# Products with values in rounds of eight chunks, for the narrow heads of a fused two-layer transformer kernel

## The chip, the cores and the metric

The kernel runs on one core of a Trainium2 chip. The metric is device time in microseconds (us), the median of several executions. The engines are PE (TensorE: matrix products), DVE (VectorE), ACT (ScalarE), POOL (GpSimd) and SP (SyncE, which issues the DMAs). Results of PE land in eight PSUM banks of 128 partitions by 512 float32; the other engines work mostly in SBUF.

## The reference

Two layers on x of shape (2, 1024, 128), each an attention with 16 heads, a layer norm, and a second block; the last block holds another attention, with heads of width 4:

```
x = layernorm(x + attention0(x))            # causal, heads of width 8
x = layernorm(x + moe0(x))                  # 8 experts, top 2, relu
x = layernorm(x + attention1(x))            # causal, heads of width 8, low rank q and k
# last block: attention2 (not causal), then 8 experts, top 2, gelu
scores = einsum('bhsk,bhtk->bhst', Q[..., :4], K) / sqrt(4)
attn   = softmax(scores); ao = einsum('bhst,bhtv->bhsv', attn, V)    # V of width 4
x = layernorm(x + block(x))
```

## The kernel before

There are 96 heads in order: 0 to 31 are attention 0, 32 to 63 attention 1 (both causal) and 64 to 95 attention 2, the narrow ones (two sequences of 16 heads). Run 0 is heads 0 to 31, followed by the experts of the first layer; run 1 is heads 32 to 95, followed by the experts of the second.

The score matrix of a head (1024 by 1024) is made twice, in chunks of one PSUM bank (128 x 512). `scores_by_query` (L1243, product at L1258) puts queries on the partitions; DVE takes the row maxima from it (`find_max`, L974, reduction at L989). The maxima are negated, split into three bf16 parts on POOL, turned to rows on PE (`max_rows`, L1278) and loaded into the operand of the keys. `scores_by_key` (L1264, product at L1273) makes the scores again with keys on the partitions and the maximum already taken off; ACT writes the exponential to SBUF (L873, into `probs`); `probs_by_v` (L1284, product at L1302) multiplies it by the values of the head, in float32, into one accumulating bank `SUM`. A value operand has 32 columns, so each product fills one of four column quarters of the array, and the quarter is chosen by the chunk's number modulo four; four successive chunks of a narrow head lie side by side in the array. When a group of heads is done (four narrow heads, two or three causal ones), ACT copies `SUM` (`take_sums`), PE turns it (`turn_sums`, L1308, L1312), ACT and POOL gather it and DVE divides it (`normalise`, L999).

A narrow head has 16 chunks, a causal one 9. The query side runs two heads ahead of the key side (`AHEAD`), so head g's loop on PE issues one query product of head g+2 and one key product of head g for each chunk; the pair occupies different rows of the array. Query products go through three banks (`S1`), and a product waits until DVE has reduced the one three before it. Key products go through another three (`S2`) and wait for ACT in the same way. The queues of all engines are written out by hand, in program order; `head` (L1387) is the PE queue of one head. Its 16 chunks stand in four batches of four. After each batch comes a round of products with values, for the four chunks of the batch before: after batch 0 the last round of the head before, after batches 1, 2 and 3 the rounds 0, 1 and 2 of this head. `turn_sums` comes after batch 1 of a head that follows a group's end, ahead of its round; `max_rows` after batch 0, ahead of its round; and other steps of the layers (projections, transposes, routing; the lists `BETWEEN`, L184 to L306) in the middle of a batch, at its second chunk on PE, its third on ACT and DVE.

`probs` has nine places of 512 columns. A narrow head uses eight (`probs_place`, L129); ACT waits before an exponential for the round that read its place last (`pv_before`, L144). The semaphore `pv` counts rounds. The causal heads have two rounds of nine products, over five and four chunks.

Of the kernel before, what the change touches and what calls it, by code (L numbers as in the profile page):

```python
# [14 lines left out]
P = 128  # L15
# [5 lines left out]
NH = B * H  # L21
# [3 lines left out]
CH = 512  # L25
# [17 lines left out]
class Attention:  # L43


    def __init__(self, layer, head_dim, scale_dim, causal):
        self.layer = layer
        self.hd = head_dim
        self.width = H * head_dim
        self.rows = PARTS * PARTS * head_dim  # L50
        self.dv = head_dim + 1

        self.groups = (3, 3, 3, 3, 2, 2) if causal else (4, 4, 4, 4)
        self.scale = float(scale_dim) ** -0.5
        self.causal = causal
        if causal:

            diagonal = [[(i, i, 1) for i in range(4 * c, 4 * c + 4)] for c in range(2)]
            self.by_query = diagonal + [
                [(7, 0, 4)], [(7, 4, 3), (1, 0, 1)], [(6, 0, 4)], [(6, 4, 2), (2, 0, 2)],  # L60
                [(5, 0, 4)], [(5, 4, 1), (3, 0, 3)], [(4, 0, 4)]]
            self.maxima = 3

            self.by_key = [
                [(i, i, 1, 3) for i in range(4)], [(0, 4, 4, 0)], [(1, 4, 4, 1)], [(2, 4, 4, 2)],
# [3 lines left out]
            self.masked = (0, 5)  # L69
            self.batches = [range(0, 5), range(5, 9)]  # L70

            self.pv_order = [
                [(1, 0), (2, 0), (3, 0), (4, 0), (0, 0), (4, 1), (0, 1), (0, 2), (0, 3)],
                [(6, 0), (8, 0), (7, 0), (8, 1), (5, 1), (5, 0), (7, 1), (5, 2), (5, 3)]]
            self.adds = 3
        else:
            self.by_query = [[(i, 4 * c, 4)] for i in range(TB) for c in range(2)]
            self.maxima = 2
            self.by_key = [[(j, 4 * half, 4, 2 * half + j % 2)] for two in range(0, TB, 2) for half in range(2)
                           for j in range(two, two + 2)]  # L80
            self.masked = ()
            self.batches = [range(c, c + 4) for c in range(0, 16, 4)]
            self.pv_order = [[(c, 0) for c in batch] for batch in self.batches]
            self.adds = 1
        self.chunks = len(self.by_key)

# [7 lines left out]
class Head:  # L94
# [32 lines left out]
        return next(k for k, batch in enumerate(self.a.batches) if c in batch)  # L127

    def probs_place(self, c):  # L129
        return c if self.a.causal else c % 8  # L130


HEADS = [Head(g) for g in range(3 * NH)]
RUNS = (range(0, NH), range(NH, 3 * NH))
CHUNKS = [sum(hd.a.chunks for hd in HEADS[:g]) for g in range(3 * NH + 1)]
BATCHES = [sum(len(hd.a.batches) for hd in HEADS[:g]) for g in range(3 * NH + 1)]
GROUP = [sum(hd.ends_group for hd in HEADS[:g]) for g in range(3 * NH + 1)]
GROUPS = [[hd for hd in HEADS if GROUP[hd.g] == i] for i in range(GROUP[-1])]
V_BEFORE = {hd.g: max((o.g for o in HEADS[:hd.g] if o.a.causal == hd.a.causal and o.v_slot == hd.v_slot), default=None)
# [3 lines left out]

def pv_before(g, c):  # L144

    if not HEADS[g].a.causal and c >= 8:
        return BATCHES[g] + (c - 8) // 4 + 1
    if g == 0:
        return 0
    if HEADS[g - 1].a.causal:  # L150
        return BATCHES[g - 1] + HEADS[g - 1].batch_of(c) + 1
    return BATCHES[g - 1] + (c + 8) // 4 + 1


def queries_upto(run, g, c):
# [169 lines left out]
def build(nc, inp, out):  # L325
    ctx = ExitStack()
    with ctx:
        def sb(name, shape, dt=F32):
            return ctx.enter_context(nc.sbuf_tensor(name, shape, dt))
# [18 lines left out]
        qk = sb("qk", [P, RING, 2, S], BF16)  # L348
        v_all = [sb("v8", [P, NH, TB, 9]), sb("v4", [P, NH, TB, 5])]
        v_heads = [sb("v_head8", [P, 6, TB, Q]), sb("v_head4", [P, RING, TB, Q])]  # L350
        probs = sb("probs", [P, 9, CH])
        sums = sb("sums", [P, 2, CH])
        by_quarter = sb("by_quarter", [P, 2, 4, 4, 27])
        pairs = sb("pairs", [P, 4, 27])
# [228 lines left out]
        def _(pool):  # L583
# [79 lines left out]
            def take_v(g):  # L663
                hd = HEADS[g]
                a = hd.a
                if V_BEFORE[g] is not None:
                    pool.wait_ge(sem("pv"), BATCHES[V_BEFORE[g] + 1])
                if a.layer == 0 and hd.n == 0:
                    pool.wait_ge(sem("v_first"), NCH)
                if a.layer > 0 and hd.h == 0:  # L670
                    taken(pool, "v", a.layer, BY_SEQUENCE[hd.b][-1])
                at = a.dv * hd.at_in_group
                nc.gpsimd.tensor_copy(v_head_of(a)[:, hd.v_slot, :, at:at + a.dv], v_of(a)[:, hd.n, :, :]
                                      ).then_inc(sem("v_head"), 1)
# [76 lines left out]
        def _(act):  # L751
# [98 lines left out]
                nc.scalar.activation(neg_rows[:, g % RING, :], neg_ps, ACT.Copy).then_inc(sem("neg_rows"), 1)  # L850

            def take_sums(i):
                act.wait_ge(sem("pv"), BATCHES[GROUPS[i][-1].g + 1])
                ge(act, "out", i - 1)
                nc.scalar.activation(sums[:, i % 2, :], SUM[:], ACT.Copy).then_inc(sem("sums"), 1)

# [323 lines left out]
        def _(pe):  # L1180
# [103 lines left out]
            def probs_by_v(g, k):  # L1284
                hd = HEADS[g]
                a = hd.a
                order = [(c, b, a.by_key[c][b][1] // 4, a.by_key[c][b][3]) for batch in a.pv_order for c, b in batch]
                opens = {next(m for m in order if m[2:] == hq) for hq in {m[2:] for m in order}}
                closes = {next(m for m in reversed(order) if m[2:] == hq) for hq in {m[2:] for m in order}}
                if k == 0:  # L1290
                    pe.wait_ge(sem("v_head"), g + 1)
                    if hd.first_of_group:
                        ge(pe, "sums", GROUP[g])
                pe.wait_ge(sem("probs"), CHUNKS[g] + a.batches[k][-1] + 1)
                for c, b in a.pv_order[k]:
                    if c in a.masked and (c, b) == next(y for y in a.pv_order[k] if y[0] == c):
                        pe.wait_ge(sem("masked"), 2 * g + a.masked.index(c) + 1)
                    j, q0, count, quarter = a.by_key[c][b]
                    at = P * sum(blk[2] for blk in a.by_key[c][:b])
                    half, q = q0 // 4, P * (q0 % 4)  # L1300
                    this = (c, b, half, quarter)
                    ins = mm(SUM[Q * quarter:Q * (quarter + 1), q:q + P * count], v_head_of(a)[:, hd.v_slot, j, :],  # L1302
                             probs[:, hd.probs_place(c), at:at + P * count],
                             start=this in opens and hd.first_of_group, stop=this in closes and hd.ends_group,
                             skip_group_check=True)
                ins.then_inc(sem("pv"), 1)
# [80 lines left out]
            def head(run, g, asked):  # L1387
                hd = HEADS[g]
                for k, batch in enumerate(hd.a.batches):
                    for c in batch:  # L1390

                        upto = min(queries_upto(run, g, c) + 1, CHUNKS[run.stop])
                        for i in range(asked, upto):
                            scores_by_query(i)
                        asked = upto
                        scores_by_key(g, c)
                        before = at_place_before(run, g, k)
                        if c == batch[1] and before is not None:
                            between(before)
                    if k == 0 and g + 1 < run.stop:  # L1400
                        max_rows(g + 1)
                    if k == 1 and g > run.start and HEADS[g - 1].ends_group:
                        turn_sums(GROUP[g - 1])
                    if k > 0:
                        probs_by_v(g, k - 1)
                    elif g > run.start:
                        probs_by_v(g - 1, len(HEADS[g - 1].a.batches) - 1)
                return asked

            def experts(f, last):  # L1410
# [37 lines left out]
            for f, run in enumerate(RUNS):  # L1448
                ge(pe, "y_taken", UNITS * f)
                half_way = CHUNKS[run.start + 1] + HEADS[run.start].a.chunks // 2  # L1450
                asked = CHUNKS[run.start]
                for i in range(asked, half_way):
                    scores_by_query(i)
                max_rows(run.start)
                for i in range(half_way, CHUNKS[run.start + AHEAD] + 1):
                    scores_by_query(i)
                asked = CHUNKS[run.start + AHEAD] + 1
                for g in run:
                    asked = head(run, g, asked)
                last = run.stop - 1  # L1460
                probs_by_v(last, len(HEADS[last].a.batches) - 1)
                experts(f, GROUP[last])


# [68 lines left out]
```

## Time and profile before

| | |
|---|---|
| median of 3 runs | 1196.16 us (1196.11 to 1196.60) |
| the profiled execution: its time, its span | 1196.12 us, 1194.4 us |
| PE, DVE, ACT, POOL busy over the span | 92%, 73%, 65%, 22% |
| mean granted TensorE clock | 0.987 of full |
| narrow heads: from after batch 0 of head 64 to the end of head 93 | 706 to 1042 us |
| heads 94 and 95, without query products beside them | 1042 to 1063 us |
| experts of the second layer | 1063 us to the end |

Times in the rows are us from the start of the span, and durations in us unless marked ns. An instruction's row on PE gives a modelled end and overlaps the next one; the distance from one start to the next is what an instruction takes of the engine. Of a row of the timeline, the first number is its start, the second its duration, "x8" the number of instructions merged into it (a float32 product is recorded as two), and the bracket at its end the idle time before it with what ended it. Some records of products are missing.

### The profile page before, as it was taken

Reading aid. Unit: us, or ns where it says so; the run is one execution under the profiler, and the core shown is the slowest. Engines: PE = TensorE matmul, PEld = TensorE weight load, DVE = VectorE, ACT = ScalarE, POOL = GpSimd, SP = SyncE. Lnnn points to the kernel's source line nnn. Section 1 sums busy time; section 2 is a strip of 40 time slices with the busy share of each in tenths; the row PEclk is TensorE's granted clock in tenths of the full one; section 3 lists DMA queues with packets and bytes.
Section 4 is the critical chain, followed back from the end, with each engine's and each line's share of the span. In section 5 each row is a group of like instructions: output and inputs, shape, how many; then the busy total and the mean of one; then the engine's idle time right before and its main releaser. Section 6 shows DMA issues by size and latency. Waiting matters only on the chain. (4 is left out here: it accounts for less than half of the span.)

```text
span 1194.4 us, 24895 instructions
## 1 busy us (share of the span) xinstructions
PE 1103.6 (92%) x8850; PEld 597.5 (50%) x8850; DVE 871.2 (73%) x2061; ACT 775.9 (65%) x1547; POOL 267.1 (22%) x795
## 2 busy tenths in 40 slices
PE   8999999999999989999988998888889898899996
PEld 5566666656666646666655532222112221136774
DVE  6888878771434487888877889899999989804433
ACT  4576766666444437676676667888888788874443
POOL 4344333331112123433334321011010010100001
PEclk9999999999999999999999999999999999999998
DMA  7345331100003501343221311002111000000000
GB/s 195 82 121 142 101 82 32 42 22 1 1 1 70 121 21 33 98 103 97 61 74 37 60 37 36 18 11 37 37 36 37 11 17 11 7 1 1 10 9 18
DMA packets 39546, 57.65 MB, mean 48 GB/s; under 512 B 9392, under 2 KB 14976, under 8 KB 39040
## 3 DMA queue, kind: packets, MB, share of 16 engines
q1 hardware_dynamic: 39424, 56.06, 19.2%
q8 instruction: 71, 1.16, 0.4%
q14 instruction: 51, 0.42, 0.1%
HBM read 30.81 MB, written 24.64 MB: 46 GB/s over the span
## 5 line engine op out<-in xcount | busy, mean ns | idle before, releaser
L873 ACT ACTIVATE probs<-bank 128x512 f32<-128x512 f32 x1088 | 577.6, 600 | 228.3 <-PE bank L1273 227.3
L989 DVE TENSOR_REDUCE tile_max<-bank 128x1 f32<-128x512 f32 (+3 forms) x1152 | 613.9, 594 | 36.5 <-PE bank L1258 31.2
L1258 PE MATMUL bank<-qk 125*128 125x128 bf16 (+2 forms) x1664 | 389.1, 311 | 49.8 <-DVE tile_max L989 43.9
L1273 PE MATMUL bank<-qk 128*128 128x128 bf16 (+1 forms) x1664 | 385.3, 309 | 5.8 <-ACT probs L873 5.3
L1302 PE MATMUL bank<-probs,v_head 128*32 128x512 f32 (+3 forms) x3328 | 304.0, 454 | 0.1
L1258 PEld LDWEIGHTS bank<-qk 125*128 125x128 bf16 (+1 forms) x1664 | 132.6, 97 | 313.1 <-DVE tile_max L989 240.1
L1156 DVE SCALAR_TENSOR_TENSOR acc<-bank,gate,acc 128x128 f32<-128x128 f32 x256 | 72.0, 344 | 156.7 <-PE bank L1426 156.7
L1302 PEld LDWEIGHTS bank<-probs,v_head 128*32 128x32 f32 x3328 | 139.7, 109 | 53.8 <-issue 31.4
L1273 PEld LDWEIGHTS bank<-qk 128*128 128x128 bf16 (+1 forms) x1664 | 133.2, 97 | 57.6 <-ACT probs L873 22.1
L893 ACT ACTIVATE probs<-bank,sb_b 128x512 f32<-128x512 f32 x128 | 81.0, 684 | 117.9 <-PE bank L1415 117.9
L983 DVE TENSOR_REDUCE tile_max<-bank 128x4 f32<-128x512 f32 x128 | 87.3, 687 | 65.9 <-PE bank L1258 65.2
L1426 PEld LDWEIGHTS bank<-sb_w,probs 128*128 128x128 f32 x1024 | 123.1, 192 | 24.5 <-issue 24.0
L1426 PE MATMUL bank<-sb_w,probs 128*128 128x128 f32 x1024 | 124.7, 275 | 0.0
L1415 PE MATMUL bank<-xT,sb_w 128*128 128x512 f32 x256 | 121.0, 595 | 0.0
L714 POOL TENSOR_SCALAR_AFFINE_SELECT probs<-probs 128x512 f32<-128x512 f32 x128 | 81.2, 634 | 153.7 <-ACT probs L873 153.6
L681 POOL CAST neg_parts<-neg_max 128x8 bf16<-128x8 f32 x96 | 18.2, 189 | 325.8 <-DVE neg_max L996 325.8
L1415 PEld LDWEIGHTS bank<-xT,sb_w 128*128 128x128 f32 x256 | 43.9, 191 | 34.1 <-issue 33.8
L1253 PE MATMUL bank<-mask,ident 128*128 128x512 bf16 x128 | 50.0, 391 | 3.5 <-DVE acc L1156 1.2
L850 ACT ACTIVATE neg_rows<-bank 24x128 bf16<-24x128 bf16 x96 | 24.7, 258 | 22.6 <-PE bank L1281 22.6
L704 POOL TENSOR_TENSOR pairs<-by_quarter 128x108 f32<-128x108 f32 (+1 forms) x24 | 9.4, 393 | 124.1 <-ACT by_quarter L861 124.1
L648 POOL TENSOR_SCALAR rstd<-mean_var 128x4 f32<-128x4 f32 (+1 forms) x12 | 2.8, 236 | 146.9 <-DVE mean_var L1047 146.6
L813 ACT ACTIVATE x<-x_plus,shift,rstd 128x128 f32<-128x128 f32 x64 | 26.2, 488 | 8.3 <-POOL shift L651 8.3
(135 smaller groups left out, 635.6 us busy)
## 6 DMA issues: line engine op xcount, KB each, us to landing
qk<-qk_parts SPq DMA_DIRECT2D x160, 144.0 KB
qk_parts<-q_parts SPq DMA_DIRECT2D x48, 192.0 KB, 2.4
qk_parts<-k_parts SPq DMA_DIRECT2D x48, 192.0 KB, 3.2
qk_parts<-q_parts SPq DMA_DIRECT2D x24, 96.0 KB, 2.3
qk_parts<-k_parts SPq DMA_DIRECT2D x24, 96.0 KB, 2.9
sb_w<-in_w SPq DMA_DIRECT2D x8, 256.0 KB, 3.7
sb_w<-in_w SPq DMA_DIRECT2D x2, 1024.0 KB, 5.9
qk<-neg_rows SPq DMA_DIRECT2D x96, 6.0 KB
```

Source lines behind the costliest of these rows:

```text
L714: nc.gpsimd.affine_select(out=p, in_=p, compare_op=ALU.is_ge, fill=0.0, base=0, pattern=[[0, 4], [1, P]], channel_multiplier=-1).then_inc( ...
L873: nc.scalar.activation(probs[:, hd.probs_place(c), :], S2[i % len(S2)][:], ACT.Exp, scale=hd.a.scale).then_inc(sem("probs"), 1)
L893: nc.scalar.activation(hidden[:, m % 2, fb, :], bank[2 * (m % 2) + fb][:], ACT.Relu if f == 0 else ACT.Gelu, bias=w_sb[f"b1_{f}"][:, FB * ...
L983: ins = nc.vector.tensor_reduce(tile_max[:, hd.slot, 4 * c:4 * c + 4, 0], s1[:].rearrange("p (t k) -> p t k", k=P), AX.X, ALU.max)
L989: ins = nc.vector.tensor_reduce(tile_max[:, hd.slot, t, which:which + 1], s1[:, at:at + P * count], AX.X, ALU.max)
L1156: ins = nc.vector.scalar_tensor_tensor(acc[:, tile, :], Y[m % 2][:, P * t:P * (t + 1)], gate[:, tile, e:e + 1], acc[:, tile, :], ALU.mult, ...
L1253: mm(s1[:], ident16[:], mask16[:].rearrange("p t k -> p (t k)"), start=True, stop=False, skip_group_check=True)
L1258: ins = mm(s1[:, at:at + P * count], qk[hd.query_rows, hd.place, 0, P * t:P * (t + 1)], qk[hd.query_rows, hd.place, 1, P * k0:P * (k0 + co ...
L1273: ins = mm(s2[:, at:at + P * count], qk[hd.key_rows, hd.place, 1, P * j:P * (j + 1)], qk[hd.key_rows, hd.place, 0, P * q0:P * (q0 + count) ...
L1302: ins = mm(SUM[Q * quarter:Q * (quarter + 1), q:q + P * count], v_head_of(a)[:, hd.v_slot, j, :], probs[:, hd.probs_place(c), at:at + P * ...
L1415: ins = mm(bank[2 * (m % 2) + fb][:], w_sb[f"w1_{f}"][:, e, P * fb:P * (fb + 1)], xT[:, tokens(c)], start=True, stop=True)
L1426: ins = mm(Y[m % 2][:, P * t:P * (t + 1)], hidden[:, m % 2, fb, P * t:P * (t + 1)], w_sb[f"w2_{f}"][:, e, fb, :], start=fb == 0, stop=fb = ...
```

## The change

For narrow heads alone, `pv_order` holds two rounds of eight chunks in place of four rounds of four, and `pv_behind` sets where round 0 goes: after batch 2. The other, round 1, goes after batch 0 of the next head (as the causal heads' does already). The causal heads keep their two rounds and their places. `probs` grows from nine to twelve places, and a narrow chunk's place is its number over all narrow heads modulo twelve; `pv_before` follows. `BATCHES`, which counted batches for the semaphore `pv`, becomes `ROUNDS`.

```diff
+            self.pv_behind = 1
...
-            self.pv_order = [[(c, 0) for c in batch] for batch in self.batches]
+
+            self.pv_order = [[(c, 0) for c in range(8 * i, 8 * i + 8)] for i in range(2)]
+            self.pv_behind = 2
...
     def probs_place(self, c):
-        return c if self.a.causal else c % 8
+        return c if self.a.causal else (16 * self.n + c) % 12
...
-BATCHES = [sum(len(hd.a.batches) for hd in HEADS[:g]) for g in range(3 * NH + 1)]
+ROUNDS = [sum(len(hd.a.pv_order) for hd in HEADS[:g]) for g in range(3 * NH + 1)]
...
-    if not HEADS[g].a.causal and c >= 8:
-        return BATCHES[g] + (c - 8) // 4 + 1
-    if g == 0:
-        return 0
-    if HEADS[g - 1].a.causal:
-        return BATCHES[g - 1] + HEADS[g - 1].batch_of(c) + 1
-    return BATCHES[g - 1] + (c + 8) // 4 + 1
+    if HEADS[g].a.causal:
+        return ROUNDS[g - 1] + HEADS[g - 1].batch_of(c) + 1 if g else 0
+    at = 16 * HEADS[g].n + c - 12
+    if at >= 0:
+        return ROUNDS[2 * NH + at // 16] + at % 16 // 8 + 1
+    return ROUNDS[g - 1] + HEADS[g - 1].batch_of(c) + 1 if c < 9 else ROUNDS[g - 1]
...
-        probs = sb("probs", [P, 9, CH])
+        probs = sb("probs", [P, 12, CH])
...
-                pe.wait_ge(sem("probs"), CHUNKS[g] + a.batches[k][-1] + 1)
+                pe.wait_ge(sem("probs"), CHUNKS[g] + max(c for c, _ in a.pv_order[k]) + 1)
...
-                    if k > 0:
-                        probs_by_v(g, k - 1)
-                    elif g > run.start:
-                        probs_by_v(g - 1, len(HEADS[g - 1].a.batches) - 1)
+                    if k == hd.a.pv_behind:
+                        probs_by_v(g, 0)
+                    elif k == 0 and g > run.start:
+                        probs_by_v(g - 1, 1)
```

## Rows read from the trace of the kernel before

**Rows 1.** The page, busy time of each engine over the span.
```profile
PE 1103.6 (92%) x8850; PEld 597.5 (50%) x8850; DVE 871.2 (73%) x2061; ACT 775.9 (65%) x1547; POOL 267.1 (22%) x795
```
**Rows 2.** Windows, narrow heads: busy by engine, granted clock, DMA share, GB/s.
```profile
706.00:1042.00 336.00, 293.47 (x2082) 73.24 (x2074) 315.11 (x590) 272.70 (x552) 39.55 (x166) 0.98 0.12 24
```
**Rows 3.** Groups by form, 706 to 1042: busy, mean ns, idle before, releaser.
```profile
L989 DVE TENSOR_REDUCE tile_max<-bank 128x1 f32<-128x512 f32 x477 | 298.2, 683 | 16.4 <-PE bank L1258 14.7
...
L947 DVE SCALAR_TENSOR_TENSOR rest<-bank,sb_bq,q_parts 64x512 f32<-64x512 f32 x2 | 1.5, 743 | 0.9 <-ACT q_parts L833 0.9
```
**Rows 4.** Timeline of PE, one undisturbed batch between two rounds.
```profile
828.25 1.07 PE L1302 MATMUL bank<-probs,v_head 128*32 128x512 f32 x8
829.25 0.39 PE L1258 MATMUL bank<-qk 61*128 61x512 bf16 x1
...
830.42 0.39 PE L1258 MATMUL bank<-qk 61*128 61x512 bf16 x1 [0.31 <-DVE tile_max L989]
...
830.74 1.07 PE L1302 MATMUL bank<-probs,v_head 128*32 128x512 f32 x8
```
**Rows 5.** Timeline of PE, then DVE, where a group's sums are turned.
```profile
848.29 0.39 PE L1258 MATMUL bank<-qk 61*128 61x512 bf16 x1 [0.32 <-DVE tile_max L989]
...
848.73 0.66 PE L1312 MATMUL bank<-ident,sums 128*128 128x128 f32 x4
849.32 1.06 PE L1302 MATMUL bank<-probs,v_head 128*32 128x512 f32 x8
850.32 0.39 PE L1258 MATMUL bank<-qk 61*128 61x512 bf16 x1
...
850.74 4.38 DVE L989 TENSOR_REDUCE tile_max<-bank 128x1 f32<-128x512 f32 x7 [0.71 <-PE bank L1258]
```
**Rows 6.** Timeline of PE, then DVE, around a causal round of five chunks.
```profile
701.64 0.37 PE L1258 MATMUL bank<-qk 61*128 61x512 bf16 x1
...
702.27 1.51 PE L1302 MATMUL bank<-probs,v_head 128*32 128x512 f32 x18
703.72 0.39 PE L1258 MATMUL bank<-qk 61*128 61x512 bf16 x1
...
704.14 4.99 DVE L989 TENSOR_REDUCE tile_max<-bank 128x1 f32<-128x512 f32 x8 [0.64 <-PE bank L1258]
```
**Rows 7.** Timeline of DVE, a group's division between reductions.
```profile
815.74 0.34 DVE L1004 RECIPROCAL den_inv<-total 128x32 f32<-128x32 f32 x1
...
816.12 0.29 DVE L1006 TENSOR_TENSOR a_tok<-total,den_inv 128x128 f32<-128x128 f32 x1
```
**Rows 8.** Timeline, the end of head 95.
```profile
1058.09 1.06 PE L1302 MATMUL bank<-probs,v_head 128*32 128x512 f32 x8
1059.09 0.82 PE L1273 MATMUL bank<-qk 64*128 64x512 bf16 x3
1059.51 2.06 ACT L873 ACTIVATE probs<-bank 128x512 f32<-128x512 f32 x4 [0.33 <-PE bank L1273]
1060.16 0.39 PE L1273 MATMUL bank<-qk 64*128 64x512 bf16 x1 [0.26 <-ACT probs L873]
1060.48 2.21 PE L1302 MATMUL bank<-probs,v_head 128*32 128x512 f32 x16
```
**Rows 9.** Windows with the granted clock: before a fall, in it, without one.
```profile
737.00:740.00 3.00, 1.61 (x13) 0.46 (x15) 2.96 (x10) 1.95 (x4) 0.94 (x5) 1.00 0.00 0
740.00:743.00 3.00, 3.00 (x16) 0.38 (x8) 2.13 (x4) 1.56 (x5) 0.00 (x0) 0.50 0.20 27
770.00:850.00 80.00, 70.17 (x495) 16.83 (x495) 76.25 (x136) 65.87 (x133) 11.55 (x40) 1.00 0.14 26
```
**Rows 10.** Timeline of PE, a round of four chunks at the low clock.
```profile
955.46 1.93 PE L1302 MATMUL bank<-probs,v_head 128*32 128x512 f32 x8
957.32 0.60 PE L1258 MATMUL bank<-qk 61*128 61x512 bf16 x1
```

More of the change, by code:

```diff
@@ L666, in take_v @@
                 if V_BEFORE[g] is not None:
-                    pool.wait_ge(sem("pv"), BATCHES[V_BEFORE[g] + 1])
+                    pool.wait_ge(sem("pv"), ROUNDS[V_BEFORE[g] + 1])
                 if a.layer == 0 and hd.n == 0:
@@ L852, in take_sums @@
             def take_sums(i):
-                act.wait_ge(sem("pv"), BATCHES[GROUPS[i][-1].g + 1])
+                act.wait_ge(sem("pv"), ROUNDS[GROUPS[i][-1].g + 1])
                 ge(act, "out", i - 1)
@@ L1460, in _ @@
                 last = run.stop - 1
-                probs_by_v(last, len(HEADS[last].a.batches) - 1)
+                probs_by_v(last, 1)
                 experts(f, GROUP[last])
```

## The prediction

> **What bounds the kernel now.** The page's busy shares come first: PE leads with 92% of the span [rows 1]. That share is a mean over stages, and the change touches one stage alone, the narrow heads, so the next view is that stage's window: in 336 us DVE is busy for 315.11 us (94%), PE for 293.47 us (87%), ACT for 272.70 us (81%) [rows 2]. There DVE is the bound. The groups by form say with what: 477 reductions of query scores hold 298.2 us of it, and in front of them DVE sat idle for only 14.7 us, all of it for PE [rows 3]. The timeline of PE shows the reverse side: from one round of products with values to the next it takes 830.74 - 828.25 = 2.49 us, and the last query product of the batch waits 0.31 us for DVE [rows 4]. 2.49 us is four reductions of 0.62 us. So PE has slack in each batch, and what decides is whether it is back from a round before DVE has emptied the three banks of query scores.
>
> That margin can be read. At a group's end PE issues its last query product at 848.29 and the next at 850.32; DVE starts on that one 0.42 us later, at 850.74, after 0.71 us of idleness [rows 5]. The filled banks had therefore lasted 850.74 - 0.71 - 848.29 = 1.74 us from the last query product. In an ordinary batch the same distance is 0.32 us (830.42 to 830.74) until the round starts, 1.00 us for the round (828.25 to 829.25) and 0.42 us until DVE starts: 1.74 us [rows 4, 5]. The cover is used up exactly; whatever PE spends more between two query products, DVE loses. The transposes of rows 5 add 0.59 us (848.73 to 849.32) and cost 0.71.
>
> **The change part by part.** *A longer round.* A round of eight puts two chunks in each column quarter, 1024 columns in place of 512. The trace has a round between these: the causal one over five chunks has at most 768 columns in a quarter and takes 703.72 - 702.27 = 1.45 us [rows 6], against 1.00 us for 512. So 256 columns cost 0.45 us, and 1024 take 1.90 us. DVE then idles 0.32 + 1.90 + 0.42 - 1.74 = 0.90 us for each. Bounds: if the second four chunks cost as much as a round of their own, the round takes 2.00 us and DVE idles 1.00; from below, the causal round shows 0.64 us of idleness where the same reckoning (2.08 + 0.42 - 1.74) gives 0.76 [rows 6], so 0.78. I take 0.90. Rounds with query products behind them are 30 (round 0 of heads 64 to 93) and 29 (round 1 of heads 64 to 92): 59 x 0.90 = +53.1 us (46 to 59).
>
> *Rounds left out.* The batches 1 and 3 have no round behind them any more. That frees PE 1.00 us each, but DVE reduces at its own rate and cannot make up a lost bank: nothing is gained. The one exception is the turn of the sums, which stood ahead of such a round and is now alone; 0.59 us of transposes are less than a round and the cover holds them. There are eight group ends in the stretch, at 0.71 us: -5.7 us (0 to -5.7) [rows 5].
>
> *Work that DVE does at the right moment.* Where DVE has other work between two reductions just before a long round, the banks last longer. The division of a group's sums comes after the reductions of batch 0; it holds DVE from 815.74 to 816.41, some 0.5 us of it not beside the reductions [rows 7]: eight times, -4.0 us. Of the steps of `BETWEEN` on DVE in these heads, six fall into a batch 0 or 2 (by their places in the list), of up to 0.74 us each [rows 3] and one longer, the routing: about -4 us. Bounds for both: 0, and 14 x 0.90 = -12.6.
>
> *Places of the exponentials, and waits.* A chunk's place was last read twelve chunks before. For chunks 4 to 11 of a head that is round 1 of the head before, issued after batch 0, and for 12 to 15 round 0, issued after batch 2: in both cases the round stands on PE ahead of the very key product that the exponential needs, so ACT gets no new wait. The wait of a round for its last exponential is met too: the key products of the batch between could not be issued otherwise. `take_sums` on ACT waits for a round that ends 0.9 us later; behind it stand exponentials whose banks are empty at that time anyway. The values' slots (POOL) are freed a head earlier than needed. No DMA moves. All this: 0.
>
> *Heads 94 and 95.* Without query products ACT is the next limit: 2.06 us for four exponentials, with 0.33 us idle after each round, a period of 1060.48 - 1058.09 = 2.39 us [rows 8]. With rounds of eight, the fourth key product goes out 1.07 us after PE is back (1059.09 to 1060.16), four more at 0.515 us each, the round 0.32 us later and PE is back after 1.90 us more: 5.35 us in place of 4.78, four times, +2.3 us. The last round waits for the last exponential (some 2.5 us after PE is back) and then takes 1.90 us, 4.4 us in place of 3.6 (1059.09 to 1062.69): +0.8. Together +3.1 us (2 to 4).
>
> Sum so far: 53.1 - 5.7 - 4.0 - 4.0 + 3.1 = +42.5 us.
>
> *The clock.* The granted clock is an unknown that this sum leaves out. Between 737 and 740 us DVE made the query products come one by one and PE was busy for 1.61 us of 3; in the 3 us behind, the granted clock was 0.50, 1.2 GHz. In the 80 us from 770, with the pattern of rows 4, it was 1.00 [rows 9]. After the change, of eight query products between two rounds three go out at once and five follow at DVE's 0.62 us, with 0.39 us of PE in each and no round for four microseconds, close to what the engine did before 740. If the clock falls there, the next long round runs at 1.2 GHz: four chunks take 957.32 - 955.46 = 1.86 us in place of 1.00 [rows 10], eight up to 3.6 in place of 1.90, and DVE idles up to 1.7 us more; the dense round then brings it back, so at most every second round is hit. Bounds: none (0) and 30 x 1.7 = +51. I take one in four, 15 x 1.7 = +25.5 us, the middle between the two, as the pattern lies between the two rows and nearer the one with a fall.
>
> The Trainium skill (TensorE: Matmul & The Clock Gate, "A second HAM failure mode: psum-queue depth-cycling") says that small idle gaps of PE between groups of products, from cycling through PSUM banks, can make the clock swing between its levels; the rows from 737 to 743 agree, and by it the time would lie with the cases that have falls.
>
> Total: 42.5 + 25.5 = +68 us. The profiled execution took 1196.12 us (its span and 1.7 us around it), the median is 1196.16, so one sum serves both: 1264 us.
>
> **The rivals.** *No further falls of the clock* (0.22): every product as above, PE at 2.4 GHz. 1196 + 42.5 = 1239, from 1230 to 1245. For it: the long round itself is dense work. Against: rows 9.
>
> *Every second round is hit* (0.12): 1239 + 51 = 1290, from 1280 to 1296. For it: all sections between rounds look alike. Against: transposes and projections lie in many of them.
>
> *The stalls are mostly hidden* (0.05): more of DVE's own work than I count meets the long rounds, or banks last longer, as in rows 6: 1200 to 1230, at 1218.
>
> *Faster* (0.04): PE's own time is the bound, not the depth of three banks. Two rounds of four take 2.00 us and one of eight 1.90, so 64 rounds save 6.4 us, and the turns 5.7: 1184 us. It holds only if PE is back before the banks are empty, that is if a round takes under 1.00 us for eight chunks, or if DVE's 94% in rows 2 is waiting that the profile hides. Rows 5 speak against it. The Trainium skill (Perfetto Trace Analysis, "Matmul Optimizations") asks for products executed back-to-back in batches, which the change does for the values; by that rule alone it would come out here, and rows 5 and 6 show what it costs another engine.
>
> *No change that can be measured* (0.02): gains and stalls cancel.
>
> **How the numbers follow.** The forecast case, with one round in ten to four in ten at the low clock, has 0.55: 1245 to 1280, likeliest 1264. The range 1232 to 1288 holds this case, most of the first rival and the near part of the second; about 0.18 lies outside. A difference of 0.2% (2.4 us) is about what a measurement can tell from none. Slower by more: 0.55 + 0.22 + 0.12 + 0.05 = 0.94; faster 0.04; same 0.02.
>
> **What would show it.** In the changed profile each round of eight should take 1.9 us from its start to the next query product, with DVE idle about 0.9 us behind it; idleness before L989 should grow from 14.7 us to some 60 to 90; the 0.71 us behind the turned sums should be gone; PE's busy share should fall; and the granted clock should be 0.5 in pieces that cover some of the rounds. The prediction is wrong if a round of eight is far from 1.9 us, if DVE is idle for less than 0.5 us behind it, or if the clock stays at 1.00 (then 1239) or falls at every other round (then 1290).

## The result and the profile after

The changed kernel takes 1252.07 us (median of 4 runs, 1248.9 to 1253.01) against 1196.38 us for the kernel before on the same chip: 1.0456 times, with a 95% interval of 1.044 to 1.0472. It is 55.7 us slower. The forecast was 1264 us, with a range of 1232 to 1288.

| | before | after |
|---|---|---|
| span of the profiled execution | 1194.4 us | 1247.2 us |
| the stretch: from the round after batch 0 of head 64 (at its `max_rows`) to the same place of head 94 | 338.5 us | 382.0 us |
| from there to the end | 150.7 us | 159.9 us |
| idle in front of the reductions of query scores, in that stretch | 16.4 us | 62.9 us |

The windows of the stretch (columns as in [rows 2]) and the group of the reductions (as in [rows 3]) in the profile after:

```profile
706.00:1087.00 381.00, 315.34 (x2079) 88.80 (x2071) 312.42 (x591) 273.39 (x555) 40.41 (x169) 0.95 0.10 21
```

```profile
L991 DVE TENSOR_REDUCE tile_max<-bank 128x1 f32<-128x512 f32 x477 | 295.2, 682 | 62.9 <-PE bank L1260 62.7
```

DVE does the same 477 reductions and is busy for about as long (3 us less, see below); what grew is the idle time in front of them, nearly all of it for PE, by 46.5 us. PE did not become the bound: its share fell from 87% to 83%. Two things are in that wait. The first is seen in any ordinary long round. The timeline of PE, then of DVE, after (the lines answer to [rows 4] and [rows 5]):

```profile
865.85 0.39 PE L1260 MATMUL bank<-qk 61*128 61x512 bf16 x1 [0.21 <-DVE tile_max L991]
...
866.16 1.92 PE L1304 MATMUL bank<-probs,v_head 128*32 128x512 f32 x16
868.02 0.39 PE L1260 MATMUL bank<-qk 61*128 61x512 bf16 x1
...
871.79 0.39 PE L1260 MATMUL bank<-qk 61*128 61x512 bf16 x1 [0.21 <-DVE tile_max L991]
...
872.12 1.93 PE L1304 MATMUL bank<-probs,v_head 128*32 128x512 f32 x16
873.99 0.39 PE L1260 MATMUL bank<-qk 61*128 61x512 bf16 x1
```

```profile
868.45 1.89 DVE L991 TENSOR_REDUCE tile_max<-bank 128x1 f32<-128x512 f32 x3 [0.86 <-PE bank L1260]
...
872.85 0.34 DVE L1006 RECIPROCAL den_inv<-total 128x32 f32<-128x32 f32 x1
873.23 0.29 DVE L1008 TENSOR_TENSOR a_tok<-total,den_inv 128x128 f32<-128x128 f32 x1
...
874.41 4.88 DVE L991 TENSOR_REDUCE tile_max<-bank 128x1 f32<-128x512 f32 x8 [0.29 <-PE bank L1260]
```

The round holds PE from 866.16 to 868.02, 1.86 us, and DVE stands idle for 0.86 us behind it. Behind the next one, where DVE has a group's division to do, it is 0.29 us. The second thing is a long round at the low clock, as here (PE and DVE):

```profile
858.77 3.48 PE L1304 MATMUL bank<-probs,v_head 128*32 128x512 f32 x16
...
862.18 0.49 PE L1260 MATMUL bank<-qk 61*128 61x512 bf16 x1
...
862.71 1.89 DVE L991 TENSOR_REDUCE tile_max<-bank 128x1 f32<-128x512 f32 x3 [2.53 <-PE bank L1260]
...
863.79 0.66 PE L1314 MATMUL bank<-ident,sums 128*128 128x128 f32 x4
```

This round takes 3.41 us and costs DVE 2.53. The window over it shows the granted clock, and beside it stands one over another such round:

```profile
855.00:862.00 7.00, 5.81 (x33) 1.23 (x27) 5.05 (x9) 4.39 (x9) 0.94 (x5) 0.79 0.09 14
889.00:893.00 4.00, 3.79 (x20) 0.69 (x18) 1.99 (x4) 1.31 (x3) 0.00 (x0) 0.59 0.00 1
```

Of the 59 rounds with query products behind them, 11 lie wholly or partly at the low clock (the round then takes 3.2 to 3.6 us, ten of them with 1.9 to 3.1 us of idle DVE), and so do the four rounds of heads 94 and 95. In the kernel before, 4 rounds of the stretch did. The turn of the sums at 863.79 no longer has a stall of its own, as it has in [rows 5]. The prediction had assumed that at most every second round can be hit. That does not hold everywhere: the rounds at 978.44 and 987.85 are neighbours, and the four of the last heads follow each other.

### The profile page after: what moved, and what is told of

The parts are those of the page before. It is cut to its first block and busy times, and to the rows that moved or that the text cites. A ratio compares the mean times of both kernels' runs of the same rounds, so it can differ in the third digit from the quotient of the medians.

```text
span 1247.2 us, 24895 instructions
## 1 busy us (share of the span) xinstructions
PE 1131.7 (91%) x8850; PEld 616.1 (49%) x8850; DVE 868.3 (70%) x2061; ACT 774.4 (62%) x1547; POOL 268.3 (22%) x795
## 5 line engine op out<-in xcount | busy, mean ns | idle before, releaser
L1260 PE MATMUL bank<-qk 125*128 125x128 bf16 (+2 forms) x1664 | 398.5, 311 | 74.9 <-DVE tile_max L991 68.4
L1275 PE MATMUL bank<-qk 128*128 128x128 bf16 (+1 forms) x1664 | 396.0, 309 | 4.8 <-ACT probs L875 2.8
L1304 PE MATMUL bank<-probs,v_head 128*32 128x512 f32 (+3 forms) x3328 | 311.4, 479 | 1.1 <-ACT probs L875 1.1
L1260 PEld LDWEIGHTS bank<-qk 125*128 125x128 bf16 (+1 forms) x1664 | 137.5, 97 | 319.2 <-DVE tile_max L991 216.0
L1304 PEld LDWEIGHTS bank<-probs,v_head 128*32 128x32 f32 x3328 | 149.9, 112 | 81.5 <-issue 68.0
L1275 PEld LDWEIGHTS bank<-qk 128*128 128x128 bf16 (+1 forms) x1664 | 138.0, 97 | 60.6 <-ACT probs L875 17.6
```

The lines of the kernel that those rows point to most:

```text
L1260: ins = mm(s1[:, at:at + P * count], qk[hd.query_rows, hd.place, 0, P * t:P * (t + 1)], qk[hd.query_rows, hd.place, 1, P * k0:P * (k0 + co ...
L1275: ins = mm(s2[:, at:at + P * count], qk[hd.key_rows, hd.place, 1, P * j:P * (j + 1)], qk[hd.key_rows, hd.place, 0, P * q0:P * (q0 + count) ...
```

## The experiments

Seven kernels were run, beside the kernel before each time (1194.68 us for the first four, 1196.87 us for the last three). "The stretch" is the one of the table above: 338.5 us before, 382.0 us after.

**The places alone.** The changed kernel with four rounds of four, one after each batch as before:

```diff
-            self.pv_order = [[(c, 0) for c in range(8 * i, 8 * i + 8)] for i in range(2)]
-            self.pv_behind = 2
+            self.pv_order = [[(c, 0) for c in range(4 * i, 4 * i + 4)] for i in range(4)]
+            self.pv_behind = 1
...
-        return ROUNDS[2 * NH + at // 16] + at % 16 // 8 + 1
+        return ROUNDS[2 * NH + at // 16] + at % 16 // 4 + 1
...
-                    if k == hd.a.pv_behind:
-                        probs_by_v(g, 0)
-                    elif k == 0 and g > run.start:
-                        probs_by_v(g - 1, 1)
+                    if k > 0:
+                        probs_by_v(g, k - 1)
+                    elif g > run.start:
+                        probs_by_v(g - 1, len(HEADS[g - 1].a.pv_order) - 1)
...
```

> The changed kernel with its twelve places and new waits, but with four rounds of four chunks after every batch as before. Theory (the length of a round against the cover of three banks of query scores): nothing of this is on DVE's path, 1196 us, within 2 us of before. Rival (the places, the address of the tiles behind them, or the waits for rounds cost time): 1200 to 1250 us.

1195.49 us, 1.0009 times before (0.9995 to 1.0023). The stretch is 338.9 us, DVE idles 16.9 us in it. The places, their waits and the memory behind them cost nothing that can be measured.

**The kernel before with other work of the same length.** `again(g, c, times)`, new here, makes the first key product of chunk c as often as it is told, once ACT has freed its bank; the right product overwrites it later.

```diff
...
+                    if not hd.a.causal and k in (0, 2):
+                        again(g, 4 * (k + 1), 5)
```

> The kernel before, rounds of four kept. Behind the rounds after batches 0 and 2 of a narrow head PE makes the first key product of the next chunk five times more (it is overwritten by the right one), about 0.86 us of PE in which no query product goes out, as much as a long round adds; PE has 1.7 us more work in each head and no work less. Theory: DVE idles about 0.86 us behind 60 rounds (+52), less some 7 us where DVE has other work, plus 3 us in heads 94 and 95, and the clock falls no more often than before, as PE is denser: 1240 to 1246 us. Rival (PE has slack of 13% in this stretch, so the filler goes into it, and the loss of the change comes from the eight-chunk round itself): 1196 to 1205 us.

1246.93 us, 1.0429 times before (1.0409 to 1.0449), a little above what was expected. The stretch grows to 385.9 us. The idle time in front of the reductions (group as in [rows 3]):

```profile
L989 DVE TENSOR_REDUCE tile_max<-bank 128x1 f32<-128x512 f32 x479 | 300.8, 683 | 62.3 <-PE bank L1258 59.0
```

Every round still has four chunks, and DVE idles about 0.88 us where the extra products stand, as behind a long round. That the sum is nearly the one of the changed kernel is partly chance: here the granted clock is low at hardly any round (mean 0.99 in the stretch), but the turns of the sums still have their stalls. PE's share of slack in the stretch is no room for work between two query products, be it a round or something else. The rival falls.

**The changed kernel with its sparse part filled.** 

```diff
+                        if not hd.a.causal and c in (1, 2, 3, 7, 8, 9, 10, 11, 15):
+                            again(g, c, 1)
                         for i in range(asked, upto):
                             scores_by_query(i)
```

`again` is the one of the run before: this chunk's key product once more, ahead of its query product.

> The changed kernel; in the sparse part between two long rounds PE makes one more key product per chunk (chunks 1, 2, 3, 7 to 11 and 15 of a narrow head) while it would wait for DVE. Theory (the low clock follows the sparse part): no falls of the granted clock among the long rounds, 11 low rounds at 1.65 us and some 6 us of the tail come back while DVE's idle 0.87 us behind each round stays: 1228 to 1238 us. Rival (the falls have another cause, or the extra products delay DVE): 1250 us or more, with as many falls as now.

1236.00 us, 1.0349 times before (1.0325 to 1.0374): with more work on PE the kernel is 14 to 16 us faster than the changed one (41.3 us above the kernel before beside it, against 55.7; 16.1 by the medians as they stand). Of the 59 long rounds one is left at the low clock (it took 2.87 us), and none in the last two heads, where the time to the end falls from 159.9 to 154.3 us. The other rounds take 1.86 us and cost DVE 0.86 to 0.88 us as before, but a dozen of them about 1.2 and three 1.5 to 1.7; some of these stand where an extra product waits for ACT behind the copy of the sums. In the stretch:

```profile
706.00:1078.00 372.00, 342.47 (x2332) 105.12 (x2329) 311.16 (x588) 273.02 (x551) 40.15 (x170) 0.99 0.11 22
```

The mean granted clock is 0.99 where it was 0.95. What PE did in the sparse part decides the clock here, and the clock is worth some 15 us of the 56.

**Half exponentials, with three and with four banks for query scores.** The base for the test of the cover makes half of each exponential in narrow heads and leaves zeros in the other half of `probs`; the test adds the change of the banks:

```diff
+            constant(nc.gpsimd.memset(probs[:], 0.0))
...
-                        nc.scalar.activation(probs[:, hd.probs_place(c), :], S2[i % len(S2)][:], ACT.Exp,
+                        wide = CH if hd.a.causal else CH // 2
+                        nc.scalar.activation(probs[:, hd.probs_place(c), 0:wide], S2[i % len(S2)][:, 0:wide], ACT.Exp,
```

```diff
-        S1 = [bank[0], bank[1], bank[6]]
-        S2 = [bank[2], bank[3], bank[5]]
+        S1 = [bank[0], bank[1], bank[6], bank[5]]
+        S2 = [bank[2], bank[3]]
...
+            pe.wait_ge(sem("v_first"), NCH)
```

> The changed kernel, but in narrow heads ACT makes only the first half of each exponential (the other half of probs stays at zero), so that ACT cannot be the limit; banks stay at three for query scores and three for key scores. It is the base for the next run. Both theories: DVE still idles 0.87 us behind each long round, the stretch from batch 0 of head 64 to batch 0 of head 94 stays at 380 to 384 us; the last two heads get some 3 to 6 us shorter: 1243 to 1250 us.

> As the run before (half exponentials in narrow heads), with four banks for query scores and two for key scores. Theory (the length of a round against the cover of the banks that DVE has filled): the cover grows by one reduction, 0.62 us, so DVE idles 0.25 us behind a long round in place of 0.87; the stretch of narrow heads gets about 37 us shorter, 340 to 350 us, with fewer falls of the clock. Rival (DVE idles for what PE's round does, whatever is filled, or the place of the round counts): the stretch stays at 375 us or more. What two key banks do to the causal heads is not part of the test.

The wait at the end of the second edit stands ahead of the first run: the values of attention 0 pass through bank 5, which the query scores now share.

With three banks 1238.9 us, below the 1243 to 1250 that were expected, mostly for what lies behind the stretch (8.5 us shorter, not 3 to 6); the stretch is 379.5 us, where both theories had 380 to 384, and DVE idles 0.86 us behind an ordinary round. With four banks the stretch is 350.8 us, 28.7 us shorter, and just above the expected 340 to 350. The round is the same 1.86 us; DVE's idleness is not. Timeline of DVE and PE (with one weight load, PEld) with four banks:

```profile
857.41 0.39 PE L1262 MATMUL bank<-qk 61*128 61x512 bf16 x1
857.94 0.09 PEld L1285 LDWEIGHTS bank<-ident,neg_parts 128*24 128x24 bf16 x1 [0.44 <-POOL neg_parts L691]
857.95 1.93 PE L1306 MATMUL bank<-probs,v_head 128*32 128x512 f32 x16
...
860.24 4.88 DVE L993 TENSOR_REDUCE tile_max<-bank 128x1 f32<-128x512 f32 x8 [0.50 <-PE bank L1262]
...
862.78 0.39 PE L1262 MATMUL bank<-qk 61*128 61x512 bf16 x1
863.10 1.92 PE L1306 MATMUL bank<-probs,v_head 128*32 128x512 f32 x16
864.96 0.39 PE L1262 MATMUL bank<-qk 61*128 61x512 bf16 x1
...
865.38 1.89 DVE L993 TENSOR_REDUCE tile_max<-bank 128x1 f32<-128x512 f32 x3 [0.27 <-PE bank L1262]
```

0.27 us behind one ordinary round of a head, as computed (0.25), and 0.50 behind the other. There the round starts 0.54 us after the last query product and not 0.32, since the turn of the maxima ahead of it waits for POOL (`neg_parts`); the banks last 2.33 us from that product in both cases, 0.59 us more than with three. Some 20 of the 28.7 us come from these shorter stalls. The other 8 or so are the clock's: 4 rounds lie at the low one, where it was 12 with three banks. The rival, that the length or the place of the round decides whatever is filled, falls. The whole kernel takes 1229.64 us; the edit costs some 20 us ahead of the stretch, which begins at 726 us and not at 706. Of these 2.4 us are there from the first reduction on, behind the added wait.

**Four banks with whole exponentials.** The same two lines of banks, and the wait with them, in the changed kernel.

> The changed kernel with all exponentials whole, four banks for query scores and two for key scores. Theory: now ACT's cover is two banks, 1.03 us, against 0.32 + 1.86 + 0.42 = 2.60 us, so ACT idles 1.6 us behind each long round and needs 8 x 0.515 us besides, 5.7 us for eight chunks, as much as the 5.75 us now: the stall moves from DVE to ACT and the stretch stays at 375 to 390 us. Rival (the query banks alone decide): 340 to 350 us.

1289.67 us; the stretch is 393.4 us, a little over the expected range. The stall is on both engines now, here behind a round that follows a turn of the sums:

```profile
889.55 1.92 PE L1304 MATMUL bank<-probs,v_head 128*32 128x512 f32 x16
891.41 0.39 PE L1260 MATMUL bank<-qk 61*128 61x512 bf16 x1
...
891.83 1.29 DVE L991 TENSOR_REDUCE tile_max<-bank 128x1 f32<-128x512 f32 x2 [1.29 <-PE bank L1260]
891.87 1.08 ACT L875 ACTIVATE probs<-bank 128x512 f32<-128x512 f32 x2 [1.61 <-PE bank L1275]
```

With ACT at full length, a bank taken from it is no gift to DVE: PE's queue is one, a key product that waits for ACT holds the query products behind it, and the banks for them stay unfilled. DVE idles 0.93 us behind one ordinary round of a head and 1.05 behind the other, against 0.86 to 0.88 with three banks, and 1.29 at a place like the one shown. Ten of the 59 rounds lie at the low clock, one fewer than in the changed kernel.

**The turn of the sums moved.** If the cover is exhausted exactly in every batch, the kernel before loses 0.71 us at a group end for no need:

```diff
                         if c == batch[1] and before is not None:
                             between(before)
-                    if k == 1 and g > run.start and HEADS[g - 1].ends_group:
-                        turn_sums(GROUP[g - 1])
+                        turn = k == 1 and g > run.start and HEADS[g - 1].ends_group
+                        if turn and not hd.a.causal and c == batch[2]:
+                            turn_sums(GROUP[g - 1])
...
-                    if k == 1 and g > run.start and HEADS[g - 1].ends_group:
+                    if turn and hd.a.causal:
+                        turn_sums(GROUP[g - 1])
```

> The kernel before, with the turn of a narrow group's sums put ahead of the last pair of score products of batch 1 instead of behind it, so that it no longer adds to the time of the round. Theory: PE waits 0.31 us for DVE at that place anyway, so 0.3 us of the transposes' 0.59 is hidden and DVE idles 0.3 to 0.4 us in place of 0.71, eight times: 1192.5 to 1194.5 us. Rival (what counts is PE's sum over the batch, which is the same): 1196 us.

1191.75 us, 0.9963 times before (0.9949 to 0.9977), the fastest kernel here by a small margin, and a little below the expected 1192.5 to 1194.5. Where [rows 5] had 0.71 us, the timeline of PE and DVE now shows:

```profile
844.58 0.66 PE L1312 MATMUL bank<-ident,sums 128*128 128x128 f32 x4
845.16 0.39 PE L1258 MATMUL bank<-qk 61*128 61x512 bf16 x1
...
845.48 1.07 PE L1302 MATMUL bank<-probs,v_head 128*32 128x512 f32 x8
846.48 0.39 PE L1258 MATMUL bank<-qk 61*128 61x512 bf16 x1
...
846.91 4.38 DVE L989 TENSOR_REDUCE tile_max<-bank 128x1 f32<-128x512 f32 x7 [0.23 <-PE bank L1258]
```

and the group of the reductions has 11.3 us of idleness in place of 16.4:

```profile
L989 DVE TENSOR_REDUCE tile_max<-bank 128x1 f32<-128x512 f32 x476 | 297.6, 683 | 11.3 <-PE bank L1258 9.6
```

The stalls at the turns make up 3.4 of the 5.1 us; the rest lies mostly around the places where the clock was low. PE has the same work in that batch; only the distance between two query products changed, and with it the time.

## Why the prediction was right, and where its sizes were off

*The bound and the cover.* Right, and shown from three sides: other work of the same length in the kernel before costs the same, a fourth bank takes away 0.59 us of an ordinary round's 0.86, and the turn of the sums at another place gives back two thirds of its own. The round of eight was put at 1.90 us and measured 1.86; DVE's idleness at 0.90 and measured 0.86 to 0.88. With 59 rounds at 0.87 this term is 51.3 us, not 53.1. One reading behind it was a little off: the cover of 1.74 us is not used up exactly in the kernel before, but missed by 0.09 us behind many rounds of four (see what the sum lacked). And the 14.7 us of idle time that it read off [rows 3] are the part that PE ended; the whole is 16.4.

*Work of DVE at the right moment.* The division: 0.87 - 0.29 = 0.58 us a time, not 0.5, though in the first two groups 0.39 and 0.53 us of idleness are left; 4.3 us, not 4.0. The steps of `BETWEEN` were put at -4 us; three rounds (at 773.5, 802.1 and 978.4 us) have no idleness at all behind them and three have 0.7, but others have 0.95 to 1.1 us in place of 0.87, and at full clock 1.4 us is left of the term. It was over-sized: steps on PE in the same batches make the stall longer, and the reckoning had only those on DVE.

*The turn of the sums.* Nothing is idle behind it any more, as forecast. It was worth 5.3 us and not 5.7: six of the eight stalls were 0.71 us, the others 0.79 and 0.20.

*What the sum lacked.* Two gains. Of the 16.4 us of idleness before, 11.1 us were not at the turns: 5.1 at the low clock, and 6 elsewhere, mostly where steps of the layers on PE lay ahead of a round of four. Of the latter 1 us is left, since half of the batches have no round behind them. And DVE's busy time in the stretch fell by 3.2 us (316.3 to 313.1). The trace of the kernel before shows what that is. These are the reductions around the first round of [rows 4]; the first row holds two, at 828.39 and 828.99:

```profile
828.39 1.28 DVE L989 TENSOR_REDUCE tile_max<-bank 128x1 f32<-128x512 f32 x2
829.67 0.69 DVE L989 TENSOR_REDUCE tile_max<-bank 128x1 f32<-128x512 f32 x1
```

A reduction lasts 0.68 us, but the next one starts 0.60 us after it if its bank is full. The one at 829.67 starts 0.69 us after the one before, and 0.42 us after PE's first query product behind the round (829.25), the distance that it has behind a stall. DVE has waited, and the profile shows no idle time for it. In the stretch that happens 42 times before and three times after: 39 x 0.087 = 3.4 us. So the 0.62 us of the prediction (2.49 us for four) is no rate of DVE, but 0.60 with a short wait in it. "Nothing is gained" by leaving out rounds was the step that failed, by some 8 us.

*Heads 94 and 95.* Forecast +3.1 us. Measured +9.2, of which 5.6 go away with the filled sparse part; the +3.6 us that stay are close to the forecast. The step left out the clock there: all four rounds ran at the low one.

*The clock.* The mechanism is shown by the filled sparse part. The size was too high. One round in four at the low clock was forecast: 15, at 1.7 us, +25.5. Measured: 11 of 59 in the stretch, together 16.2 us above what they would cost at full clock, and 5.6 us in the last heads, less the 5.1 us that the rounds at the low clock had cost before: +16.7 us. The forecast did not take off these four, and it took every low round as fully exposed, while the one at 978 us is hidden behind DVE's routing.

Together: +51.3 - 4.3 - 1.4 - 5.3 - 5.0 - 3.2 + 3.6 + 16.7 = +52.4 us against 52.8 us between the two spans. Without the clock the sum comes to 35.7 us where the prediction had 42.5, and the clock to 16.7 where it had 25.5: both parts were too high, and of the second the prediction could say only that it lay between 0 and 51. So the forecast missed the measured time by 12 us and the rival without falls (1239) by 13; what decides between them is the clock in the traces, not the total. The forecast case, a stall of 0.9 us behind each long round and a clock that falls at a part of them, was the right one. The first rival, without falls, would have given 1239, close to what the filled kernel takes (1236); the second needed about every other round at the low clock. The rival on the other side needed PE as the bound.

Of the two rules of the Trainium skill weighed ahead of the result, the one on idle gaps that come from cycling through PSUM banks (TensorE: Matmul & The Clock Gate, "A second HAM failure mode: psum-queue depth-cycling") agrees with the mean granted clock of 0.95 after, 0.98 before and 0.99 with the sparse part filled. The one on products back-to-back in batches (Perfetto Trace Analysis, "Matmul Optimizations") would have had it faster by itself, and the measurement decides against it here: the longer batch starved the engine that was the bound, and left PE too sparse between two batches.

## What to carry to other kernels

Where one engine feeds two others from one queue, the longest stretch without a product for the bound engine has to be shorter than what its filled banks last, here 0.32 + round + 0.42 us against 1.74 us (by estimate 1.65, the 0.09 us less, if the bound engine is to lose nothing at all); the feeder's slack over the stage says nothing on it. Read that margin at a place where something extra already stands in the queue, and put extra steps where the feeder waits anyway, not next to its longest round. Do not take a row without idle time for proof that the bound engine did not wait: compare the distance between two starts. A long round has a second price if it leaves the rest sparse: the clock may be low just when the round comes.

## What the runs showed of the hardware

A reduction of a full bank starts 0.60 us after the one before, while one that had to wait for its bank starts when the one before is through, 0.68 us after it or later (0.69 at 829.67 in the kernel before). So a wait of less than 0.1 us shows as busy time.

In the kernel before with filler, the extra key products and the query products behind them in program order use different rows of the array, and in the records the first query product starts ahead of the last three extra ones. Yet DVE does not start on the first of them until all five extra products are through. PE's and DVE's timeline there (L1285 is the extra product):

```profile
871.15 0.60 PE L1285 MATMUL bank<-qk 64*128 64x512 bf16 x2
871.39 0.39 PE L1258 MATMUL bank<-qk 61*128 61x512 bf16 x1
871.59 0.38 PE L1285 MATMUL bank<-qk 64*128 64x512 bf16 x1
871.61 0.38 PE L1258 MATMUL bank<-qk 61*128 61x512 bf16 x1
871.81 0.38 PE L1285 MATMUL bank<-qk 64*128 64x512 bf16 x1
871.83 0.38 PE L1258 MATMUL bank<-qk 61*128 61x512 bf16 x1
872.03 0.38 PE L1285 MATMUL bank<-qk 64*128 64x512 bf16 x1
...
872.45 1.89 DVE L989 TENSOR_REDUCE tile_max<-bank 128x1 f32<-128x512 f32 x3 [0.88 <-PE bank L1258]
```

The query product starts at 871.39, and with the usual 0.42 us DVE would start at 871.81; it starts at 872.45, 0.42 us after the start of the last extra product. Starts pass each other between disjoint rows, while what waits for a product is let go in program order. That is read from records, and no run isolates it.
